# Split-precision pointwise product, stacked half slice in the down product, and a reordered first chunk, in a fused recurrent + FP4 feed-forward kernel

## The chip, the cores and the metric

One core of one Trainium2 chip. The metric is device time in microseconds (us) of one execution: the median of three runs is given, and beside it the span of one profiled execution, from its first to its last instruction.

## The reference

The input x has 16 sequences of 512 tokens with 256 features. With xn = layernorm(x), the kernel computes x + s * silu(f). All matrices are applied on the feature axis.

```python
# s: the recurrent branch
h  = dwconv3(rmsnorm(xn, g0)) + b           # 3 causal taps for each feature
x1 = h @ pw.T + b_pw + xn                   # "pointwise", 256 x 256
hidden, gate = split(rmsnorm(x1, g1) @ gru.T)          # 256 -> 512
x2 = minGRU(hidden, gate) + x1              # h_t = (1-z_t) h_(t-1) + z_t g(hidden_t)
s  = gelu(rmsnorm(x2, g2) @ w1.T + b1) @ w2.T + b2 + x2    # 256 -> 1024 -> 256
# f: the FP4 branch; q4 rounds to E2M1 in blocks of 16 with a scale for each block
hid = silu(q4(xn) @ q4(w_gate).T) * (q4(xn) @ q4(w_up).T)  # 256 -> 704
f   = q4(hid) @ q4(w_down).T                               # 704 -> 256
```

## The kernel before

A chunk is one sequence of 512 tokens; there are 16. `first()` does the first chunk and prepares the weights, `body(c, front)` is run for chunks 1 to 15 (`front` is false in the last), and `tail(15)` finishes. Every engine has its own hand-written order of steps (`first`, `body`, `tail` in each block), is strictly in order, and waits on semaphores. The loops are unrolled. In `body(c)` the FP4 branch's second half (quantise the hidden, transpose, `down`) and the second feed-forward product (`ff2`) of chunk c-1 run between `gate_up`, `gru` and `ff1` of chunk c; at the end of `body(c)` the front of chunk c+1 is made (`front_xc`, `front_xq`, `pointwise`).

Products that need near-float32 precision are made of float32r parts: each operand is held as a high part (ACT casts it to float32r) and a remainder (DVE subtracts), and `product` issues three matmuls: high x high, high x remainder, remainder x high. Only `pointwise` used plain float32 operands (`pw`, `y`): `product` then issues one float32 matmul, which the profile shows as two records. The names of a step's parts: `xs_hi/xs_lo` and `xslo_ready`, `act_hi/act_lo`, `xq_hi/xq_lo`, `hqt_hi/hqt_lo` and `hqtlo_ready`.

The 704 hidden features are five full slices of 128 and one half slice of 64 (`NFULL` = 5, `LAST` = 64, `KI` = 6). `hq` rows are 768 long, with zeros behind the 704 (set by POOL at the start), so that `down` runs six slices of 128 rows, 18 matmuls of 256 columns for each tile t of 128 tokens. DVE's steps for a tile are `hidden` (silu times up, L496), `fp4_scales`, `fp4_ratios`, `fp4_round`, `hidden_values` (L427, writes `hq`) and `hidden_low` (L519, writes `hqt_lo`).

The second rmsnorm of a chunk is a chain: DVE `recurrence` (both halves, L551 to L559), ACT `squares`, DVE `add_squares` (L524), PE `sum_squares` (L1042), DVE `clamp_sums` (L529, L531), POOL `rms_scale` (L348), PE `spread_scale` (L1050), DVE `scaled` (L539), ACT `high_part` (L799), DVE `scaled_low` (L545), PE `ff1`.

In `first()`, weights are quantised in six steps (`weight(0..5)` transposes, `weight_rest` subtracts the high part; `down_weight`, `down_rest` for the down matrix). `keep_busy(n)` issues n matmuls of the identity with no use but activity. The remainders of the gru, w1 and w2 weights are made by POOL (`low_weights`, L363).

Of the kernel before, what the change touches and what calls it, by code (L numbers as in the profile page):

```python
# [27 lines left out]
P = 128  # L28
# [31 lines left out]
def mixed_recurrent_kernel(nc, x, columns, pw_t, gru_t, w1_t, w2_t, w_gate, w_up, w_down, identity, out):  # L60
# [15 lines left out]
    with ctx:  # L76
# [17 lines left out]
        minus_ident = sb("minus_ident", [P, P], F32R)  # L94
# [7 lines left out]
        pw = sb("pw", [P, KD, D])  # L102
# [43 lines left out]
        w2_f, act_hi = shared_home(("w2_f", [P, KF * D + KD * NI], F32), ("act_hi", [P, KF, L], F32R))  # L146
# [5 lines left out]
        hqt_lo = sb("hqt_lo", [P, KI, P], F32R)  # L152
# [13 lines left out]
        dn_rows = w2_f[:, KF * D:KF * D + KD * NI].rearrange("p (k n) -> p k n", k=KD)  # L166
        w2_f = w2_f[:, 0:KF * D].rearrange("p (a n) -> p a n", a=KD)
        gru_f = keep[:, :, 0:2 * D]
# [12 lines left out]
        constants_ready = sem("constants_ready")  # L181
# [3 lines left out]
        wlo_ready = sem("wlo_ready")  # L185
        wq_ready = sem("wq_ready")
# [17 lines left out]
        y_ready = sem("y_ready")  # L204
        xqhi_ready = sem("xqhi_ready")
# [182 lines left out]
        def _(dve):  # L388
# [96 lines left out]

            def front_fp4_low(c):
# [28 lines left out]
            def hidden_low(c, t):  # L515
# [3 lines left out]
                V.tensor_tensor(hqt_lo[:], hqt_ps, hqt_hi[:].bitcast(F32), ALU.subtract).then_inc(hqtlo_ready, 1)  # L519
# [83 lines left out]
            def down_weight(e):  # L603

                if e == 0:
                    dve.wait_ge(constants_ready, 1)
                    dve.wait_ge(ld_dn, 16)
                dve.wait_ge(wqm_done, NFULL + e)
                quantise(dn_rows[:, e, :], hq[:, e, 0:NI], NBI).then_inc(wq_ready, 1)
# [3 lines left out]
            def first():  # L613
                front_moments(0)
                front_rows(0)
                front_fp4_values(0, front_fp4_ratios(0))
                front_taps(0)
                weight_values(0, weight_ratios(0, weight_scales(0)))
# [12 lines left out]
                scales = weight_scales(4)  # L631
                add_squares(1)
                weight_values(4, weight_ratios(4, scales))
                clamp_sums(1, gu_ps[:, 0, 0, :])
                weight_values(5, weight_ratios(5, weight_scales(5)))
                scaled(1, x1, gu_ps[:, 0, 1, :], (x2_ready, KD))
                scaled_low(1)
                down_weight(0)
# [9 lines left out]
                hidden(0, 3)  # L648
                ratios = fp4_ratios(hid[:, 0, :], NBI, hidden_scales(0, 0))
# [3 lines left out]
                hidden_low(0, 0)  # L653
                carried["ratios"] = fp4_ratios(hid[:, 1, :], NBI, hidden_scales(0, 1))
# [673 lines left out]
```

## Time and profile before

| what | value |
|---|---|
| median of 3 runs | 1087.53 us (1085.81 to 1088.24) |
| profiled execution: own time | 1085.26 us |
| profiled execution: span | 1083.5 us |
| granted TensorE clock, mean | 0.997 of full speed |
| PE / DVE / ACT / POOL busy | 1061.8 / 934.5 / 607.3 / 147.5 us |

A busy share tells how full an engine is; a view by time tells which of the engines a given wait ends on. Both are used below.

### The profile page before, as it was taken

How to read it: one execution, taken by the hardware profiler on the slowest of the kernel's cores; microseconds unless marked ns; L12 is line 12 of the kernel's file. 1: busy time of each engine (PE TensorE's matmuls, PEld its weight loads, DVE VectorE, ACT ScalarE, POOL GpSimd, SP SyncE). 2: the span in 40 equal slices, each digit the busy share in tenths (PEclk: the TensorE clock that was granted, in tenths of full speed). 3: DMA queues.
4: the chain of work that ended last, by engine and by line, in shares of the span. 5: the costliest groups of instructions: out<-in, count | busy, mean ns of one | idle time of the engine just before them, and what ended most of it. 6: DMA issues, size and time to landing. Idle time of an engine off the chain costs nothing. (4 is left out here: it accounts for less than half of the span.)

```text
span 1083.5 us, 18319 instructions
## 1 busy us (share of the span) xinstructions
PE 1061.8 (98%) x6954; PEld 967.9 (89%) x6954; DVE 934.5 (86%) x1720; ACT 607.3 (56%) x967; POOL 147.5 (14%) x123
## 2 busy tenths in 40 slices
PE   7899999999999999999999999999999999999998
PEld 6788989989898998989999898998989899898998
DVE  6978988989888898988889898898989889898895
ACT  5564464564746547474654747455574645647452
POOL 1230101112020110201111010111101011120010
PEclk9999999999999999999999999999999999999999
DMA  7000001010010101001010010101001010100110
GB/s 248 1 21 1 1 2 59 1 60 1 1 59 1 59 1 47 13 2 59 1 60 1 21 40 1 59 1 60 1 1 59 1 59 1 59 1 2 39 40 21
DMA packets 29365, 31.45 MB, mean 29 GB/s; under 512 B 1120, under 2 KB 28512, under 8 KB 29280
## 3 DMA queue, kind: packets, MB, share of 16 engines
q1 hardware_dynamic: 28448, 29.43, 8.7%
q8 instruction: 56, 0.92, 0.4%
q10 hardware_dynamic: 832, 0.87, 0.2%
q14 instruction: 29, 0.24, 0.1%
HBM read 21.90 MB, written 8.39 MB: 28 GB/s over the span
## 5 line engine op out<-in xcount | busy, mean ns | idle before, releaser
L990 PE MATMUL gu_ps<-gu_hi,xq_hi 128*128 128x352 f32 x512 | 168.3, 329 | 0.0
L990 PE MATMUL gu_ps<-gu_lo,xq_hi 128*128 128x352 f32 x512 | 165.9, 324 | 0.0
L990 PE MATMUL gu_ps<-gu_hi,xq_lo 128*128 128x352 f32 x512 | 165.7, 324 | 0.0
L990 PE MATMUL w_ps<-w_hi,act_hi 128*128 128x256 f32 x480 | 140.1, 292 | 0.0
L990 PE MATMUL w_ps<-w_hi,act_lo 128*128 128x256 f32 x480 | 135.1, 281 | 0.0
L990 PE MATMUL w_ps<-w_lo,act_hi 128*128 128x256 f32 x480 | 134.9, 281 | 0.0
L990 PE MATMUL w_ps<-dn_hi,hqt_hi 128*128 128x256 f32 x384 | 116.6, 304 | 2.0 <-DVE hqt_lo L519 2.0
L990 PE MATMUL w_ps<-dn_hi,hqt_lo 128*128 128x256 f32 x384 | 108.5, 283 | 0.0
L990 PE MATMUL w_ps<-dn_lo,hqt_hi 128*128 128x256 f32 x384 | 108.4, 282 | 0.0
L818 ACT ACTIVATE g<-w_ps 128x256 f32<-128x256 f32 x64 | 24.7, 385 | 147.7 <-PE w_ps L990 147.6
L496 DVE TENSOR_TENSOR hid<-sl,gu_ps 128x704 f32<-128x704 f32 x64 | 56.8, 887 | 58.8 <-PE gu_ps L990 58.2
L990 PE MATMUL gu_ps<-xs_hi,w_hi 128*128 128x512 f32 x256 | 102.5, 400 | 0.4 <-DVE xs_lo L545 0.4
L990 PE MATMUL gu_ps<-xs_lo,w_hi 128*128 128x512 f32 x256 | 101.0, 395 | 0.0
L990 PE MATMUL gu_ps<-xs_hi,w_lo 128*128 128x512 f32 x256 | 101.0, 395 | 0.0
L990 PEld LDWEIGHTS gu_ps<-gu_hi,xq_hi 128*128 128x128 f32 x512 | 96.7, 189 | 0.2 <-issue 0.2
L990 PEld LDWEIGHTS gu_ps<-gu_lo,xq_hi 128*128 128x128 f32 x512 | 96.6, 189 | 0.0
L990 PEld LDWEIGHTS gu_ps<-gu_hi,xq_lo 128*128 128x128 f32 x512 | 96.3, 188 | 0.0
L842 ACT ACTIVATE act<-gu_ps,cols 128x512 f32<-128x512 f32 x128 | 86.1, 687 | 13.7 <-PE gu_ps L990 13.3
L812 ACT CAST hqt_hi<-w_ps 128x768 fp32r<-128x768 f32 x64 | 51.3, 802 | 73.0 <-PE w_ps L1058 72.2
L356 POOL TENSOR_TENSOR o<-o,x_res 128x1024 f32<-128x1024 f32 x15 | 36.1, 2403 | 400.8 <-issue 393.4
L990 PEld LDWEIGHTS w_ps<-w_lo,act_hi 128*128 128x128 f32 x480 | 90.6, 189 | 0.0
L990 PEld LDWEIGHTS w_ps<-w_hi,act_hi 128*128 128x128 f32 x480 | 90.4, 188 | 0.0
(136 smaller groups left out, 2703.6 us busy)
## 6 DMA issues: line engine op xcount, KB each, us to landing
x_in<-x_dram SPq DMA_DIRECT2D x16, 512.0 KB, 5.8
x_res<-x_dram SPq DMA_DIRECT2D x16, 512.0 KB, 5.0
out_dram<-o SPq DMA_DIRECT2D x15, 512.0 KB, 3.5
act<-w_t_dram SPq DMA_DIRECT2D x1, 1024.0 KB, 11.3
w_f<-w_t_dram SPq DMA_DIRECT2D x1, 1024.0 KB, 13.8
w_f<-w_down_dram SPq DMA_DIRECT2D x1, 704.0 KB, 9.4
hid<-w_gate_dram SPq DMA_DIRECT2D x1, 640.0 KB, 5.9
hid<-w_up_dram SPq DMA_DIRECT2D x1, 640.0 KB, 9.3
```

Source lines behind the costliest of these rows:

```text
L356: nc.gpsimd.tensor_tensor(o[:], o[:], x_res[:], ALU.add).then_inc(out_ready, 1)
L496: V.tensor_tensor(hid[:, t, :].rearrange("p (h n) -> p h n", h=2), sl[:], gu_ps[:, 1, :, 0:HALF], ALU.mult).then_inc(hid_ready, 1)
L812: A.copy(hqt_hi[:], hqt_ps).then_inc(hqthi_ready, 1)
L818: A.activation(g[:, t, :], bank[:, 0:D], ACT.Silu).then_inc(g_ready, 1)
L842: A.activation(act1[:, j, :], ff1_bank(j), ACT.Gelu, bias=b1c[:, j:j + 1]).then_inc(gelu_ready, 1)
L990: done = M.matmul(psum, l, r, start=first and i == 0, stop=last and i == len(terms) - 1)
```

## The change

1. **Pointwise.** `pw` becomes `pw_hi` (cast by ACT in `first`) and `pw_lo` (subtracted by DVE in `first`); `y` gets `y_hi` (ACT, `front_y_high`) and `y_lo` (DVE, `front_y_low`) in every chunk. `pointwise` calls `product` with pairs.
2. **Down.** `hidden_values` writes the last 64 hidden features twice, into both halves of the last slice, in a second instruction. `hidden_low` leaves the remainder of the five full slices in `hqt_lo` (now five slices), and puts the half slice's remainder into rows 64 to 127 of the last slice of `hqt_hi`, in a second instruction over 64 partitions. `down` then covers the half slice with two matmuls: 64 rows of high x remainder weight, and 128 rows of (high, remainder) x (high weight, high weight). `down` has 17 matmuls.
3. **Body order.** PE does `front_xc(c + 1)` ahead of `ff1` and not in its middle. ACT does `front_y(c + 1)` after the first gelu and `front_y_high(c + 1)` ahead of the last two. DVE does `front_taps` ahead of `front_fp4_values`, then `front_y_low`.
4. **First chunk.** w1 and w2 remainders are made by DVE (`ff_low(1)`, `ff_low(2)`). Weight steps 3 to 5 move behind the second `spread_scale`, between the tiles of `ff1(0)`; `gelus_high(0, ...)` moves behind `hq_columns(0, 0)` and around `silu_f(0, 0)`; `front_xq(1)` comes ahead of `pointwise(1)`. The counts of `keep_busy` change.
5. **Homes.** `gru_f` is kept in `o`, `pw_f` behind `w2_f`, `y_hi` in `keep`'s place, `y_lo` in `cand`'s, `minus_ident` in `hqt_lo`; POOL's zeroing of `hq` is gone.

```diff
+        pw_hi = sb("pw_hi", [P, KD, D], F32R)
+        pw_lo = sb("pw_lo", [P, KD, D], F32R)
...
+        keep, y_hi = shared_home(("keep", [P, KD, L], F32), ("y_hi", [P, KD, L], F32R))
+        cand, y_lo = shared_home(("cand", [P, KD, L], F32), ("y_lo", [P, KD, L], F32R))
...
             def first():
                 layernorm_scales(0, 1)
-                low_weights(0)
+                gru_low()
                 rms_scale(0)
-                pool.wait_ge(xslo_ready, KD)
-                low_weights(1)
                 rms_scale(1)
-                pool.wait_ge(xslo_ready, 2 * KD)
-                low_weights(2)
                 layernorm_scales(1, 3)
...
+            def fp4_hidden_values(dst, rounded):
+                n, last = NBI * FP4_BLOCK, NFULL * P // FP4_BLOCK
+                fp4_values(dst[:, 0:n], NBI, rounded)
+                return V.scalar_tensor_tensor(blocks(dst[:, n:KI * P], NBI - last),
+                                              blocks(q_m[:, NFULL * P:n].bitcast(BF16), NBI - last),
+                                              1.0 / UNIT, spread(q_scale[:, last:NBI], NBI - last),
+                                              ALU.mult, ALU.mult)
...
+            def front_y_low(c):
+                for k in range(KD):
+                    dve.wait_ge(yhi_ready, KD * c + k + 1)
+                    V.tensor_tensor(y_lo[:, k, :], y[:, k, :], y_hi[:, k, :].bitcast(F32),
+                                    ALU.subtract).then_inc(ylo_ready, 1)
...
-                V.tensor_tensor(hqt_lo[:], hqt_ps, hqt_hi[:].bitcast(F32), ALU.subtract).then_inc(hqtlo_ready, 1)
+                V.tensor_tensor(hqt_lo[:], hqt_ps[:, 0:NFULL, :], hqt_hi[:, 0:NFULL, :].bitcast(F32), ALU.subtract)
+                twin = hqt_hi[LAST:P, NFULL, :]
+                V.tensor_tensor(twin, hqt_ps[LAST:P, NFULL, :], twin.bitcast(F32),
+                                ALU.subtract).then_inc(hqtlo_ready, 1)
...
+            def ff_low(j):
+                _, src, hi, lo = split_weights[j]
+                for k in range(KD):
+                    dve.wait_ge(whi_ready, KD * j + k + 1)
+                    V.tensor_tensor(lo[:, k, :], src[:, k, :], hi[:, k, :].bitcast(F32),
+                                    ALU.subtract).then_inc(flo_ready, 1)
...
             def first():
                 front_moments(0)
+                dve.wait_ge(pwhi_ready, 1)
+                V.tensor_tensor(pw_lo[:], pw_f, pw_hi[:].bitcast(F32), ALU.subtract).then_inc(pwlo_ready, 1)
                 front_rows(0)
...
-                weight_values(0, weight_ratios(0, weight_scales(0)))
+                scales = weight_scales(0)
+                front_y_low(0)
+                weight_values(0, weight_ratios(0, scales))
...
-                ratios = weight_ratios(2, weight_scales(2))
+                scales = weight_scales(2)
                 scaled(0, x1, w_ps[:, 1, :], (x1_ready, KD))
+                ratios = weight_ratios(2, scales)
+                scaled_low(0)
                 weight_values(2, ratios)
-                scaled_low(0)
-                weight_values(3, weight_ratios(3, weight_scales(3)))
+                ff_low(1)
                 recurrence(0, 0)
                 recurrence(0, 1)
...
                 hidden(0, 3)
+                front_y_low(1)
...
                 hidden_low(0, 0)
+                ff_low(2)
                 carried["ratios"] = fp4_ratios(hid[:, 1, :], NBI, hidden_scales(0, 1))
...
-                    front_fp4_values(c + 1, front_fp4_ratios(c + 1))
+                    ratios = front_fp4_ratios(c + 1)
                     front_taps(c + 1)
+                    front_fp4_values(c + 1, ratios)
+                    front_y_low(c + 1)
...
+            def front_y_high(c):
+                for k in range(KD):
+                    act.wait_ge(y_ready, KD * c + k + 1)
+                    act.wait_ge(pw_done, KD * c)
+                    act.wait_ge(x2_ready, KD * c)
+                    A.copy(y_hi[:, k, :], y[:, k, :]).then_inc(yhi_ready, 1)
...
                 hq_columns(0, 0)
+                gelus_high(0, range(KF // 2))
                 silu_f(0, 0, w_ps[:, 2, :])
+                gelus_high(0, range(KF // 2, KF))
...
-                for j in range(KF // 2):
+                gelus(c, (0,))
+                if front:
+                    front_y(c + 1)
+                gelus_high(c, (0,))
+                for j in range(1, KF // 2):
                     gelus(c, (j,))
                     gelus_high(c, (j,))
                 if front:
-                    front_y(c + 1)
-                    gelus(c, range(KF // 2, KF))
+                    gelus(c, range(KF // 2, KF - 2))
+                    front_y_high(c + 1)
+                    gelus(c, range(KF - 2, KF))
...
-                    pe.wait_ge(y_ready, KD * (c + 1))
+                    pe.wait_ge(yhi_ready, KD * (c + 1))
+                    pe.wait_ge(ylo_ready, KD * (c + 1))
...
-                        last = product(w_ps[:, e, :], pw[:, k, e * P:(e + 1) * P], y[:, k, :], False, k == KD - 1)
+                        last = product(w_ps[:, e, :], (pw_hi[:, k, e * P:(e + 1) * P], pw_lo[:, k, e * P:(e + 1) * P]),
+                                       (y_hi[:, k, :], y_lo[:, k, :]), False, k == KD - 1)
...
-                for k in range(KI):
-                    last = product(bank[:, 0:D], (hqt_hi[:, k, :], hqt_lo[:, k, :]),
-                                   (dn_hi[:, k, :], dn_lo[:, k, :]), k == 0, k == KI - 1)
-                last.then_inc(dn_done, 1)
+                for k in range(NFULL):
+                    product(bank[:, 0:D], (hqt_hi[:, k, :], hqt_lo[:, k, :]), (dn_hi[:, k, :], dn_lo[:, k, :]),
+                            k == 0, False)
+                M.matmul(bank[:, 0:D], hqt_hi[0:LAST, NFULL, :], dn_lo[0:LAST, NFULL, :], start=False, stop=False)
+                M.matmul(bank[:, 0:D], hqt_hi[:, NFULL, :], dn_hi[:, NFULL, :], start=False,
+                         stop=True).then_inc(dn_done, 1)
...
                 ff2(c - 1, 2, w_ps[:, 2, :], (g_ready, T * c))
-                ff1(c, range(KF // 2))
                 if front:
                     pe.wait_ge(sg_ready, T * c - 2)
                     front_xc(c + 1)
+                ff1(c, range(KF // 2))
+                if front:
                     ff1(c, range(KF // 2, KF))
```

## Rows read from the trace of the kernel before

**Rows 1.** The page: engine, busy us (share of the span), instructions.
```profile
PE 1061.8 (98%) x6954; PEld 967.9 (89%) x6954; DVE 934.5 (86%) x1720; ACT 607.3 (56%) x967; POOL 147.5 (14%) x123
```

**Rows 2.** Waits of PE: whom, us in total, times, longest.
```profile
PE gu_ps L1050 <- POOL inv_rms L348: 3.0, 14, 0.2
PE gu_ps L1109 <- issue: 1.7, 1, 1.7
```

**Rows 3.** Timeline of PE, pointwise, chunk 7: start us, us, engine, line, instruction.
```profile
545.58 0.60 PE L1013 MATMUL w_ps<-ident,xn 128*128 128x128 f32 x4
546.01 1.88 PE L990 MATMUL w_ps<-cand,pw 128*128 128x512 f32 x4
547.73 0.60 PE L1013 MATMUL w_ps<-ident,xn 128*128 128x128 f32 x4
```

**Rows 4.** Timeline of PE, a `down` of 18, then `gru`; a product behind transposes.
```profile
507.82 0.28 PE L990 MATMUL w_ps<-dn_hi,hqt_hi 128*128 128x256 f32 x1
...
509.96 0.39 PE L990 MATMUL gu_ps<-xs_hi,gru_hi 128*128 128x512 f32 x1
...
512.05 0.39 PE L990 MATMUL gu_ps<-xs_hi,gru_hi 128*128 128x512 f32 x1
...
522.80 0.36 PE L990 MATMUL w_ps<-dn_hi,hqt_hi 128*128 128x256 f32 x1
523.00 0.27 PE L990 MATMUL w_ps<-dn_lo,hqt_hi 128*128 128x256 f32 x1
```

**Rows 5.** Timeline of DVE, chunk 7; in brackets its idle time and what ended it.
```profile
486.23 3.09 DVE L512 TENSOR_TENSOR act_lo<-act,act_hi 128x512 fp32r<-128x512 f32 x5
492.18 0.89 DVE L496 TENSOR_TENSOR hid<-sl,gu_ps 128x704 f32<-128x704 f32 x1 [2.86 <-PE gu_ps L990]
...
503.13 0.89 DVE L496 TENSOR_TENSOR hid<-sl,gu_ps 128x704 f32<-128x704 f32 x1 [0.34 <-PE gu_ps L990]
...
520.78 0.95 DVE L519 TENSOR_TENSOR hqt_lo<-w_ps,hqt_hi 128x768 fp32r<-128x768 f32 x1
521.65 0.68 DVE L524 TENSOR_TENSOR xs<-xs 128x512 f32<-128x512 f32 x1
522.25 0.42 DVE L566 TENSOR_TENSOR o<-w_ps,g 128x256 f32<-128x256 f32 x1
523.08 0.69 DVE L529 TENSOR_REDUCE ss_sum<-gu_ps 128x4 f32<-128x512 f32 x1 [0.41 <-PE gu_ps L1042]
```

**Rows 6.** Timeline of PE, second rmsnorm of chunk 7.
```profile
522.21 0.28 PE L990 MATMUL w_ps<-w_hi,act_lo 128*128 128x256 f32 x1
522.39 0.66 PE L1042 MATMUL gu_ps<-ident,xs 128*128 128x128 f32 x4
...
525.39 0.65 PE L1050 MATMUL gu_ps<-ident,inv_rms 128*128 128x128 f32 x4 [0.22 <-POOL inv_rms L348]
```

**Rows 7.** Timeline of DVE and of ACT, end of chunk 7 (front of chunk 8).
```profile
538.81 1.22 DVE L427 SCALAR_TENSOR_TENSOR xq<-q_e,q_scale 128x1024 f32<-128x1024 bf16 x1
...
541.57 1.97 ACT L842 ACTIVATE act<-gu_ps,cols 128x512 f32<-128x512 f32 x3
...
546.55 2.20 ACT L807 CAST act_hi<-act 128x512 fp32r<-128x512 f32 x4
```

**Rows 8.** Timeline of DVE, first chunk and start of the second.
```profile
36.32 1.87 DVE L403 TENSOR_SCALAR q_wide<-q_amax 128x32 f32<-128x32 f32 x1
...
42.58 0.68 DVE L551 SCALAR_TENSOR_TENSOR cand<-gu_ps,cand 128x512 f32<-128x512 f32 x1
...
119.25 0.89 DVE L496 TENSOR_TENSOR hid<-sl,gu_ps 128x704 f32<-128x704 f32 x1 [0.34 <-PE gu_ps L990]
```

**Rows 9.** Timeline of PE, first chunk: gru, ff1.
```profile
35.95 0.47 PE L990 MATMUL gu_ps<-xs_hi,gru_hi 128*128 128x512 f32 x1 [1.96 <-DVE xs_lo L545]
...
59.13 0.47 PE L990 MATMUL gu_ps<-xs_hi,w_hi 128*128 128x512 f32 x1 [0.44 <-DVE xs_lo L545]
```

**Rows 10.** Timeline of POOL, first chunk.
```profile
35.77 4.75 POOL L363 TENSOR_TENSOR w_lo<-act,w_hi 128x1024 fp32r<-128x1024 f32 x2 [5.96 <-DVE xs_lo L545]
```

More of the change, by code:

```diff
@@ L151, in mixed_recurrent_kernel @@
         hqt_hi = sb("hqt_hi", [P, KI, P], F32R)
-        hqt_lo = sb("hqt_lo", [P, KI, P], F32R)
+        hqt_lo = sb("hqt_lo", [P, NFULL, P], F32R)
         q_amax = sb("q_amax", [P, 64])
@@ L166, in mixed_recurrent_kernel @@
         dn_rows = w2_f[:, KF * D:KF * D + KD * NI].rearrange("p (k n) -> p k n", k=KD)
+        pw_f = w2_f[:, KF * D + KD * NI:KF * D + KD * NI + KD * D].rearrange("p (k n) -> p k n", k=KD)
         w2_f = w2_f[:, 0:KF * D].rearrange("p (a n) -> p a n", a=KD)
-        gru_f = keep[:, :, 0:2 * D]
+        minus_ident = hqt_lo[:, 0, :]
+        gru_f = o[:].rearrange("p t d -> p (t d)").rearrange("p (k n) -> p k n", k=KD)
         gu_rows = hid[:].rearrange("p t n -> p (t n)")[:, 0:WT * D].rearrange("p (t d) -> p t d", d=D)
@@ L883, in first @@
                 act.wait_ge(ld_const, 32)
-                A.activation(minus_ident[:], ident[:], ACT.Copy, scale=-1.0).then_inc(minus_ready, 1)
+                A.activation(minus_ident, ident[:], ACT.Copy, scale=-1.0).then_inc(minus_ready, 1)
                 act.wait_ge(small_ready, 1)
+                act.wait_ge(ld_pw, 16)
+                A.copy(pw_hi[:], pw_f).then_inc(pwhi_ready, 1)
                 front_xc(0)
@@ L889, in first @@
                 high_weights(0)
+                front_y_high(0)
                 front_xq(0)
@@ L1146, in weight_rest @@
                 for i, (hi, bank) in enumerate(places):
-                    last = M.matmul(bank, minus_ident[:], hi, start=False, stop=i == len(places) - 1)
+                    last = M.matmul(bank, minus_ident, hi, start=False, stop=i == len(places) - 1)
                 last.then_inc(wqm_done, 1)
@@ L1173, in down_rest @@
                     n = min(4, KI - k)
-                    last = M.matmul(hqt_ps[:, k:k + n, :], minus_ident[:], dn_hi[:, k:k + n, e * P:(e + 1) * P],
+                    last = M.matmul(hqt_ps[:, k:k + n, :], minus_ident, dn_hi[:, k:k + n, e * P:(e + 1) * P],
                                     start=False, stop=True)
@@ L1203, in first @@
                 weight_rest(2)
+                keep_busy(24, w_ps[:, 0, :])
+                sum_squares(1, gu_ps[:, 0, 0, :], (coef_ready, 1))
+                keep_busy(8, w_ps[:, 0, :])
+                spread_scale(1, gu_ps[:, 0, 1, :], (cand_ready, 1))
                 weight(3)
-                weight_rest(3)
-                keep_busy(20, w_ps[:, 0, :])
-                sum_squares(1, gu_ps[:, 0, 0, :], (coef_ready, 1))
-                weight(4)
-                keep_busy(7, w_ps[:, 0, :])
-                spread_scale(1, gu_ps[:, 0, 1, :], (cand_ready, 1))
-                weight_rest(4)
-                weight(5)
                 keep_busy(8, w_ps[:, 0, :])
                 pe.wait_ge(whi_ready, 2 * KD)
-                pe.wait_ge(wlo_ready, 2 * KD)
-                ff1(0, range(1))
+                pe.wait_ge(flo_ready, KD)
+                ff1(0, (0, 1))
+                weight_rest(3)
+                ff1(0, (2,))
+                weight(4)
+                ff1(0, (3,))
+                weight_rest(4)
+                ff1(0, (4,))
+                weight(5)
+                ff1(0, (5,))
                 weight_rest(5)
-                ff1(0, range(1, KF // 2))
+                ff1(0, (6, 7))
                 down_weight(0)
-                ff1(0, range(KF // 2, KF))
-                down_rest(0)
                 pe.wait_ge(wqlo_ready, NFULL + 1)
                 gate_up(0, 0, 0)
-                down_weight(1)
+                down_rest(0)
                 gate_up(0, 0, 1)
                 gate_up(0, 1, 0)
+                down_weight(1)
+                gate_up(0, 1, 1)
                 down_rest(1)
-                gate_up(0, 1, 1)
                 front_xc(1)
@@ L1232, in first @@
                     gate_up(0, t, 1)
-                pointwise(1)
                 pe.wait_ge(hid_ready, T)
                 front_xq(1)
+                pointwise(1)
                 hq_transposes(0, 0, (dnlo_ready, KD))
```

75 lines of the change are left out of this document (37 added, 38 removed).

## The prediction

> **What bounds the kernel now.** I read the page's busy shares first. PE is busy 98% of the span, DVE 86%, ACT 56% [rows 1]: time can only leave if PE's stream gets shorter or its few waits go. The waits of PE come next: in the steady chunks there is one kind, 14 waits of at most 0.2 us for POOL's inverse root [rows 2]. So a matmul taken out should show in the end, unless DVE, the second fullest engine, can't follow. That needs the timeline of one steady chunk, and there the reader is to see where DVE is ahead of PE and where it is not. It is ahead by 2.86 us at the first `hidden` of a body and by 0.34 us at the third, and from 503.13 us to 523.08 us it has no wait at all [rows 5]. At the end of that stretch its `add_squares` ends near 522.33 (0.68 us from 521.65) and PE's `sum_squares` starts at 522.39, where the pitch of the matmuls alone gives 522.33 [rows 5, 6]. So in every chunk PE and DVE arrive at the second rmsnorm together; behind it comes a fixed chain, DVE, POOL, PE, whose end at `spread_scale` PE already awaits for 0.22 us [rows 6]. I split a chunk there: stretch A from `spread_scale` over the front of the next chunk to the third `hidden`, set by PE; stretch B from the third `hidden` to `spread_scale`, set by DVE and the chain.
>
> **Pointwise, PE.** One half (four transposes, two products) takes 547.73 - 545.58 = 2.15 us, 0.43 of it transposes, so two float32 products take 1.72 [rows 3]. In float32r a 512-column matmul follows the last after (512.05 - 509.96) / 9 = 0.232 us [rows 4]; six are 1.39 us. The half falls to 1.82, the chunk by 0.66 us; I take 0.64. The first float32r matmul behind transposes holds its successor up by 0.08 (523.00 - 522.80 = 0.20 for 0.12) [rows 4]; if that is not in the 0.43 already, the gain is 0.48. All of it lies in stretch A.
>
> **Down, PE.** 18 matmuls take 509.96 - 507.82 = 2.14 us, 0.119 each [rows 4]. One fewer saves 0.12 us, four times a chunk: the second of a body (tile 1 of the chunk before) and the first tile in stretch A, two in stretch B. No row shows a matmul of 64 rows. From below its extra cost is nothing, since 256 columns stream as before. The nearest row is the change from transposes to products: 0.08 us once [rows 4], which would leave 0.04 of the 0.12. From above: the array empties before and behind it; a matmul is there 0.28 us at a pitch of 0.12 [rows 4], so 0.16 for each change of form, 0.32 in all, or a loss of 0.20 for a `down`; and if the weight load (967.9 / 6954 = 0.14 us in the mean [rows 1]), otherwise overlapped, stands open at each change too, 0.60, or a loss of 0.48. I take nothing, as no change between the kinds of work in the rows costs more than 0.08, and keep both ends.
>
> The Trainium skill, TensorEngine Tiling (Array Packing), Key Properties, says that a change of tiling mode drains the engine, and a product over 64 rows may be such a change. By that rule the saving in `down` becomes the loss worked out above, the sum moves from -8.4 us to about +2; no row here can show it, every matmul stands as 128*128.
>
> **DVE's additions.** An instruction of DVE costs about 0.07 us and a column of 128 lanes about 1.04 ns: `hqt_lo` with 768 columns has a pitch of 521.65 - 520.78 = 0.87, five of 512 columns take 3.09, some 0.60 each [rows 5]. `front_y_low`: two of 512, 1.2 us a chunk, in stretch A. `hidden_values`: 64 more columns and one more instruction, 0.14 us, four times. `hidden_low`: 640 + 128 columns are the same 768, one instruction more, 0.07 us, four times. Bounds for the small ones: 0 if they overlap wholly, 0.42 each as for the shortest full-width row, `o` with 256 columns [rows 5]; the latter is hardly reached by a fourth of the columns. Together 2.0 us a chunk; DVE has 149 us idle in 16 chunks, 9 each [rows 1], so as a sum they fit. What counts is the place.
> - Stretch A: `y_low` comes where DVE then still is ahead at the first `hidden`: of 2.86 us [rows 5], 1.2 go for `y_low`, about 0.3 for the small ones and 0.88 because PE comes sooner. About 0.5 us of lead is left. Nothing lost, no wait of PE.
> - The third `hidden` has 0.34 us of lead [rows 5]; `hidden_values` takes 0.14 and the shorter `down` 0.12. It stays with PE by less than 0.1.
> - Stretch B: `hidden_low`, `hidden_values`, `hidden_low` stand between the third `hidden` and `add_squares`: 0.07 + 0.14 + 0.07 = 0.28 us, with no lead. The end of the stretch comes 0.28 later, and the two shorter `down` in it save nothing, PE waits some 0.4 us at `sum_squares` and 0.3 at `spread_scale`.
>
> **Order in the body.** `front_taps` now stands ahead of the 1.22 us `xq` values that ended at 540.03; about 3 us of taps put them at 543.2, for eight transposes that start 0.87 us (0.43 for four [rows 3]) ahead of pointwise, at 544.7. ACT's `y_high` follows the second gelu of the row at 541.57, thus 542.9, two casts of 0.55 end at 544.0 [rows 7]; `y_low` ends near 544.8, and pointwise starts at 545.58 [rows 3]. A cover of 0.8 us: if it is gone, PE waits ahead of pointwise for what is over. `front_xc` ahead of `ff1` only changes places with it. Behind PE's wait stand `down` and the next chunk's `gate_up`. No DMA moves in the body; `SP`'s queue has the same order. POOL only loses instructions; what stood behind its two subtractions (`rms_scale(1)`, the layernorm of chunk 1) waits for DVE's sums as before.
>
> **Steady sum.** Stretch A: -0.64 - 0.12 - 0.12 = -0.88; stretch B: +0.28. Together -0.60 us for each of the 13 intervals from chunk 1's `spread_scale` to chunk 14's: -7.8 us.
>
> **Last chunk.** Interval 14 to 15: -0.88, and -0.12 as DVE has no front to make there: -1.0. In the tail PE waited 1.7 us for DVE's remainders ahead of `ff2` [rows 2]; three `hidden_values` and one `hidden_low` more make that later by 0.49, and three shorter `down` behind it give 0.36 back: +0.1.
>
> **First chunk.** `pw_lo` (0.6 us) and `y_low` (1.2) are new ahead of the first rmsnorm, but two weight steps move behind it, so `gru` starts about 1.2 us later than 35.95 [rows 9]. Then POOL's 4.75 us subtraction no longer runs beside DVE [rows 10]; it stretched DVE's `q_wide` of 32 columns to 1.87 us [rows 8], where a price of 0.07 and 1.04 ns a column makes 0.1; two instructions of DVE find room in those 4.75 us, so I take 3.5 us in all. DVE's own subtraction costs 4 x 0.60 = 2.3 us. The recurrence starts at 41 to 42 for 42.58 [rows 8], a weight step of 2.7 us (three or four passes over 512 columns at 0.6 and small ones) has left the way behind it, and `ff1` starts near 56.3 for 59.13 [rows 9]. Of these 2.8 us, 1.2 go where `down_rest(0)`, before it hid between `ff1` tiles, now is PE's. Behind the gates `y_low` and the w2 subtraction (2.3) hold DVE, and ACT's eight casts of `act_hi` at 0.55 [rows 7], which formerly filled its gaps, wait for the latter: the gate's silu of chunk 1 comes last behind them, `hidden(1, 0)` is DVE's to be late with, and the third `hidden` of chunk 1 lands at 119.3 for 119.25 [rows 8]. With stretch B: +0.3 us. This walk has a dozen steps; I give it -3 to +2.
>
> **Sum.** +0.3 - 7.8 - 1.0 + 0.1 = -8.4 us. The profiled execution has a span of 1083.5 and a time of 1085.26, 2.3 below the median of 1087.53; the same difference on each gives 1075.1, 1076.9 and **1079.1 us** for the median.
>
> **Rivals.**
> 1. *DVE takes nothing back.* If `add_squares` has room that the timeline hides, PE's whole saving shows: 15 x 0.64 + 64 x 0.12 = 17.3 us, 1070. For it: PE at 98%. Against: the 20 us of DVE without a wait. It needs additions under 0.1 us.
> 2. *A small price for 64 rows*, 0.08 us: stretch A gives 0.16 less in 14 intervals, 0.3 in the tail: -5.8, 1081.7.
> 3. *The array empties* (0.32 us): `down` loses 0.20. Stretch A -0.24, stretch B still +0.28 at `sum_squares`, the next loss fits the 0.22 wait: about 0 a chunk, +1 to +2 in all: 1088 to 1090. No change.
> 4. *Slower*: emptying and an open weight load, a loss over 0.25 us for each `down`, decides; at the upper bound of 0.48 stretch A has -0.64 + 0.96 = +0.32, stretch B 0.96 less the 0.28 of waits that it has now, +0.68: 1.0 a chunk, 15 us in the steady chunks and 1 in the tail, 1103. For it: the weight loads, which have no other cover than the matmul before. Against: the switches that rows show cost 0.08.
> 5. *The first chunk is worse*, a wait for `wqm_done` or the half clock behind a gap: 3 us given up, 1082.
>
> **How the numbers follow.** Forecast as worked out 0.45; rival 1 0.11; rival 2 0.16; rival 5 0.06; rival 3 0.12; rival 4 0.10. 0.2% is 2.2 us, what this measurement can tell. Faster: 0.45 + 0.11 + 0.16 + 0.06 = 0.78; same 0.12; slower 0.10. The forecast's own range is 1076 to 1082.5 (first chunk -3 to +2, 0.48 or 0.64 for pointwise, small DVE instructions at 0 or twice the price). To leave out no more than 2 in 10, it must reach to rival 1 and to rival 3: 1070 to 1089.
>
> **What the changed profile would show.** Right: pointwise half 1.82 us; `down` 17 matmuls in 2.02 us; DVE `y_low` at 0.6; the chunk's period down by 0.60 from (503.13 - 119.25) / 6 = 63.98, the third `hidden` of chunk 7 against that of chunk 1 [rows 5, 8]; a new wait of PE at `sum_squares` of 0.3 to 0.5 us in chunks 1 to 14. Wrong: a gap beside the 64-row matmul; a wait ahead of pointwise for `y_low`; no wait at `sum_squares`; the third `hidden` of chunk 1 off 119.3 by more than 2.

## Result, and the profile after: slower by 1.1%

The changed kernel takes 1097.91 us (median of 4 runs, 1097.36 to 1100.12) beside 1087.62 for the kernel before: ratio 1.0111, 95% interval 1.0095 to 1.0126. The forecast was 1079.1, faster; even the range, up to 1089, did not hold it. The profiled execution took 1098.24 us with a span of 1096.5 at a granted clock of 0.998, 13.0 us above the span before.

The page's first part, after (engine, busy us, share, instructions), answers to [rows 1]:

```profile
PE 1072.4 (98%) x6982; PEld 981.5 (90%) x6982; DVE 976.6 (89%) x1887; ACT 618.7 (56%) x1000; POOL 138.1 (13%) x118
```

PE's busy time rose by 10.6 us although each half of pointwise became shorter and each `down` has a matmul less: something in PE's stream costs more. Its waits after (whom, us, times, longest), against [rows 2]:

```profile
PE gu_ps L1099 <- DVE xs L540: 4.1, 14, 0.3
PE gu_ps L1168 <- issue: 1.9, 1, 1.9
```

The wait at `sum_squares` (L1099) is there 14 times, as forecast, and the one for POOL's inverse root has shrunk to 0.4 us in all; 4.1 and 0.4 for the 3.0 of before, 1.5 us more and no explanation of 13. So the next view is PE's timeline. The end of one `down` in the body of chunk 7, its last four matmuls and the first of `gate_up`, with two of the weight loads (PEld):

```profile
502.40 0.28 PE L1045 MATMUL w_ps<-dn_lo,hqt_hi 128*128 128x256 f32 x1
502.40 0.19 PEld L1045 LDWEIGHTS w_ps<-dn_hi,hqt_lo 128*128 128x128 f32 x1
502.52 0.28 PE L1045 MATMUL w_ps<-dn_hi,hqt_lo 128*128 128x256 f32 x1
502.73 0.18 PEld L1125 LDWEIGHTS w_ps<-dn_lo,hqt_hi 64*128 64x128 f32 x1
502.73 0.38 PE L1125 MATMUL w_ps<-dn_lo,hqt_hi 64*128 64x256 f32 x1
503.04 0.38 PE L1126 MATMUL w_ps<-dn_hi,hqt_hi 128*128 128x256 f32 x1
503.26 0.32 PE L1045 MATMUL gu_ps<-gu_hi,xq_hi 128*128 128x352 f32 x1
```

The reader is to look at the starts, not the durations. The pitch is 0.12 us until the matmul of 64 rows; that one starts 0.21 behind its predecessor, the next 0.31 behind it, the next 0.22. Over the regular 0.12 these are 0.09, 0.19 and 0.10: **0.38 us for one matmul of 64 rows among matmuls of 128**, against the 0.12 us that the matmul taken out saves. A `down` is 0.26 us longer, not 0.12 shorter.

The weight loads say more. Inside the stream a load starts with the matmul ahead of its own, 0.12 us before it is wanted (502.40 for the matmul at 502.52). The load of the 64-row matmul starts at 502.73, together with that matmul, and the load behind it starts together with its own at 503.04; both matmuls last 0.38 us for 0.28. So at both changes the weight load stands open, which rival 4 named. How the price divides between an array that empties and an open load is not shown.

Pointwise, chunk 9 (starts of the two halves and of what follows), against [rows 3]:

```profile
615.43 0.60 PE L1069 MATMUL w_ps<-ident,xn 128*128 128x128 f32 x4
...
617.27 0.60 PE L1069 MATMUL w_ps<-ident,xn 128*128 128x128 f32 x4
...
619.12 0.28 PE L1045 MATMUL w_ps<-dn_hi,hqt_hi 128*128 128x256 f32 x1
```

A half is 1.84 us (forecast 1.82, before 2.15). Its gain of 0.62 us a chunk is there.

DVE from the third `hidden` of chunk 7 to `add_squares`, against [rows 5]:

```profile
507.40 0.89 DVE L508 TENSOR_TENSOR hid<-sl,gu_ps 128x704 f32<-128x704 f32 x1 [0.47 <-PE gu_ps L1045]
...
510.88 0.76 DVE L531 TENSOR_TENSOR hqt_lo<-w_ps,hqt_hi 128x640 fp32r<-128x640 f32 x1
511.65 0.29 DVE L534 TENSOR_TENSOR hqt_hi<-w_ps,hqt_hi 64x128 fp32r<-64x128 f32 x1
511.98 1.29 DVE L561 TENSOR_TENSOR xs_lo<-xs,xs_hi 128x512 fp32r<-128x512 f32 x2
...
516.73 0.22 DVE L435 SCALAR_TENSOR_TENSOR hq<-q_e,q_scale 128x64 f32<-128x64 bf16 x1
516.86 1.40 DVE L444 BATCH_NORM_STATS2 stats<-x_in 128x6 f32<-128x256 f32 x4
...
525.49 0.82 DVE L531 TENSOR_TENSOR hqt_lo<-w_ps,hqt_hi 128x640 fp32r<-128x640 f32 x1
526.32 0.29 DVE L534 TENSOR_TENSOR hqt_hi<-w_ps,hqt_hi 64x128 fp32r<-64x128 f32 x1
526.64 0.69 DVE L540 TENSOR_TENSOR xs<-xs 128x512 f32<-128x512 f32 x1
```

From `hidden` to `add_squares` it is 526.64 - 507.40 = 19.24 us; before, 521.65 - 503.13 = 18.52 [rows 5]. The 0.72 more: the second `hidden_low` has a pitch of 526.64 - 525.49 = 1.15 where one instruction took 0.87 (0.28 more), the first 1.10 for 0.81 there (0.29), the values 0.13. Neighbouring instructions of 128 lanes overlap by some 0.08 in most places: `hq` with 64 columns starts 0.81 after an instruction of 0.89. (Not where one reads what the one ahead wrote, as in the recurrence: 519.58 follows 518.86 by 0.72, for a duration of 0.68.) The one on 64 lanes reads nothing that its predecessor writes, and still doesn't overlap: it starts 0.77 and 0.83 after instructions of 0.76 and 0.82, and its successor 0.33 and 0.32 after it, though it has only 128 columns and lasts 0.29.

The two stretches of the prediction, from the timelines of DVE (L508, the third `hidden`) and PE (L1107, `spread_scale`):

```profile
572.24 0.89 DVE L508 TENSOR_TENSOR hid<-sl,gu_ps 128x704 f32<-128x704 f32 x1 [0.47 <-PE gu_ps L1045]
```
```profile
595.23 0.65 PE L1107 MATMUL gu_ps<-ident,inv_rms 128*128 128x128 f32 x4
```
```profile
636.88 0.89 DVE L508 TENSOR_TENSOR hid<-sl,gu_ps 128x704 f32<-128x704 f32 x1 [0.46 <-PE gu_ps L1045]
```

The period is 636.88 - 572.24 = 64.64 us (63.98 before). Stretch B is 595.23 - 572.24 = 22.99 where it was 525.39 - 503.13 = 22.26: +0.73. Stretch A is 41.65 where it was 63.98 - 22.26 = 41.72: -0.07, which is -0.62 for pointwise and about +0.54 for two `down`.

The ends of the program, third `hidden` of chunk 1 and of chunk 15:

```profile
119.61 0.89 DVE L508 TENSOR_TENSOR hid<-sl,gu_ps 128x704 f32<-128x704 f32 x1 [0.48 <-PE gu_ps L1045]
...
1024.96 0.89 DVE L508 TENSOR_TENSOR hid<-sl,gu_ps 128x704 f32<-128x704 f32 x1 [0.46 <-PE gu_ps L1045]
```

Before, the first stood at 119.25 [rows 8], and the last was

```profile
1014.95 0.89 DVE L496 TENSOR_TENSOR hid<-sl,gu_ps 128x704 f32<-128x704 f32 x1 [0.34 <-PE gu_ps L990]
```

So the 13.0 us are: first chunk +0.36; fourteen intervals, 905.35 - 895.70 = +9.65 (fourteen of 0.65 are 9.1; two intervals are 0.2 and 0.3 longer); from there to the end, 71.54 for 68.55, +3.0. In this tail PE's wait ahead of `ff2` was 1.95 us for 1.74 and ended at 1070.93 and 1060.03. The stretches of 28 matmuls behind it (the windows view: us, then busy time of each engine, the granted clock, DMA share, GB/s), first after, then before:

```profile
1071.20:1075.60 4.40, 4.40 (x28) 4.40 (x27) 4.11 (x10) 0.32 (x1) 0.00 (x0) 0.69 0.00 0
```
```profile
1060.20:1063.30 3.10, 3.10 (x28) 3.10 (x28) 3.00 (x7) 0.61 (x2) 0.00 (x0) 1.00 0.02 5
```

The granted clock has a mean of 0.69 there after the longer wait, thus part of the stretch at the level of 1.2 GHz, and 1.00 before: 4.4 us for 3.1, 1.3 of the tail's 3.0. The trace has the lower level from 1070.48, still inside the wait, to 1073.89.

The length of the wait alone is not what decides. With `down` of before and three 64-row matmuls (an experiment below) the wait at this place was 1.41 us and ended at 1074.99, and the clock fell:

```profile
1075.20:1078.60 3.40, 3.40 (x18) 3.40 (x17) 3.30 (x7) 0.90 (x2) 0.00 (x0) 0.51 0.02 5
```

With one such matmul it was 1.36 and the clock stayed at 1.00, as it did behind 1.77 in the kernel with pointwise alone, and behind the wait of 2.15 us that ends at 99.14 in the changed kernel itself.

Of the two longer intervals, that from chunk 7 to 8 can be followed. ACT, with no wait for another engine, is late by 0.28 us:

```profile
545.69 0.62 ACT L850 CAST act_hi<-act 128x512 fp32r<-128x512 f32 x1 [0.39 <-ACT act L885]
```

`y_hi`, `y_low` and pointwise (550.77) pass it on, and PE loses 0.2. The kernel with pointwise alone has the same 0.19 in the same interval. What held ACT is not shown.

### The profile page after: what moved, and what is told of

Same layout as the page of the kernel before. It is cut to its first block, busy times and chain, and to the rows that moved or that the text cites. A ratio compares the mean times of both kernels' runs of the same rounds, so it can differ in the third digit from the quotient of the medians.

```text
span 1096.5 us, 18651 instructions
## 1 busy us (share of the span) xinstructions
PE 1072.4 (98%) x6982; PEld 981.5 (90%) x6982; DVE 976.6 (89%) x1887; ACT 618.7 (56%) x1000; POOL 138.1 (13%) x118
## 4 chain that ended last, share of the span: by engine, by line
PE 68%; DVE 26%; issue 4%; DMA 1%; ACT 1%; POOL 0%; ACTq 0%; DVEq 0%
PE gu_ps L1045 35%; PE w_ps L1045 20%; DVE xs L572 3%; DVE hqt_lo L531 2%; PE w_ps L1115 2%; DVE cand L570 2%; DVE xs L555 2%; DVE stats L444 2%; DVE cand L567 2%; DVE hid L508 1%; DVE xs_lo L561 1%; DVE q_amax L402 1%; PE w_ps L1126 1%; PE w_ps L1125 1%; DVE q_y L414 1%
## 5 line engine op out<-in xcount | busy, mean ns | idle before, releaser
L1045 PE MATMUL w_ps<-dn_hi,hqt_hi 128*128 128x256 f32 x320 | 94.0, 294 | 2.6 <-DVE hqt_hi L534 2.6
L1045 PEld LDWEIGHTS w_ps<-w_hi,act_lo 128*128 128x128 f32 x480 | 90.4, 188 | 0.0
L1045 PE MATMUL w_ps<-dn_hi,hqt_lo 128*128 128x256 f32 x320 | 90.0, 281 | 0.0
L1045 PE MATMUL w_ps<-dn_lo,hqt_hi 128*128 128x256 f32 x320 | 89.9, 281 | 0.0
```

The lines of the kernel that those rows point to most:

```text
L1045: done = M.matmul(psum, l, r, start=first and i == 0, stop=last and i == len(terms) - 1)
```

## Experiments

Theory E: the 64-row matmul costs 0.38 us of PE wherever it stands (the array empties), the 64-lane subtraction 0.28 us of DVE in stretch B, and pointwise gives its 0.6 us a chunk undiminished. Rivals were that the loss is the stacking itself (its extra work on DVE, whatever the rows), and that pointwise or the new order takes its gain back. All periods below are from third `hidden` to third `hidden` in steady chunks. The kernels of one group ran together; ratios are to the kernel before in the same group (medians 1087.72, 1085.22 and 1085.86 us in the three groups), and are what may be compared across groups.

### The remainder's matmul over all 128 rows

```
-M.matmul(bank[:, 0:D], hqt_hi[0:LAST, NFULL, :], dn_lo[0:LAST, NFULL, :], start=False, stop=False)
+M.matmul(bank[:, 0:D], hqt_hi[:, NFULL, :], dn_lo[:, NFULL, :], start=False, stop=False)
```

It adds the product of the two remainders to the sum, a term that neither kernel has.

> The changed kernel with the remainder-weight product of the half slice over all 128 rows (17 matmuls, none of 64 rows). Theory (the array empties around a matmul of 64 rows, 0.38 us for each down): the last two matmuls follow at 0.12 us, a down takes 2.02 us for 2.41, the chunk's period falls from 64.63 to 63.87 us, since only the two down of stretch A save 0.38 each and stretch B stays with DVE; wait of PE at sum_squares 0.6 to 0.7 for 0.29; median 1085 to 1087. Rival (it is the in-place rows of hqt_hi, written by DVE, or the end of the group that holds the last matmuls up): gaps of 0.2 to 0.3 us remain, median 1097.

1085.85 us, ratio 0.9986 (0.9975 to 0.9998); period 63.87. PE, end of a `down` and start of `gru`, then the second rmsnorm:

```profile
573.54 0.28 PE L1125 MATMUL w_ps<-dn_lo,hqt_hi 128*128 128x256 f32 x1
573.66 0.29 PE L1126 MATMUL w_ps<-dn_hi,hqt_hi 128*128 128x256 f32 x1
573.78 0.39 PE L1045 MATMUL gu_ps<-xs_hi,gru_hi 128*128 128x512 f32 x1
...
586.98 0.66 PE L1099 MATMUL gu_ps<-ident,xs 128*128 128x128 f32 x4 [0.67 <-DVE xs L540]
```

The pitch is 0.12 throughout, though the rows written in place and the end of the group are as before: that rival is out. One matmul's row range changed, 64 rows to 128, and 12 us are gone: 64.64 - 63.87 = 0.77 a chunk, two times 0.38 in stretch A. In stretch B the price had been covered by DVE: now PE waits 0.67 us for `add_squares` where it waited 0.3.

### The remainder subtraction over 128 lanes as well

```
+V.memset(fold[0:LAST, :], 0.0)
+V.memset(fold[LAST:P, :], -1.0)
...
-twin = hqt_hi[LAST:P, NFULL, :]
-V.tensor_tensor(twin, hqt_ps[LAST:P, NFULL, :], twin.bitcast(F32), ALU.subtract)
+twin = hqt_hi[:, NFULL, :]
+V.scalar_tensor_tensor(twin, twin.bitcast(F32), fold[:, 0:1], hqt_ps[:, NFULL, :], ALU.mult, ALU.add)
```

On top of the last kernel. In this form rows 0 to 63 of the slice are written too: they get their value from PSUM once more, again as float32r.

> As rows128, and the remainder of the half slice made over 128 lanes: hi * (0 or -1 by row) + hqt_ps, so that rows 0 to 63 are rounded again and rows 64 to 127 get the remainder. Theory (an instruction over 64 lanes does not overlap its neighbours on DVE: 0.28 us more for hidden_low and not 0.07): hidden_low costs 0.87 + 0.07, stretch B shortens by 2 x 0.2 = 0.4 us, period 63.45, median 1079 to 1081. Rival (any second instruction after the first one costs 0.28): the period stays at that of rows128.

1081.64 us, ratio 0.9946 (0.9929 to 0.9962); period 63.54, each just above what was expected. DVE, a `hidden_low` in front of `add_squares`:

```profile
582.32 0.82 DVE L532 TENSOR_TENSOR hqt_lo<-w_ps,hqt_hi 128x640 fp32r<-128x640 f32 x1
583.05 0.34 DVE L535 SCALAR_TENSOR_TENSOR hqt_hi<-hqt_hi,fold,w_ps 128x128 fp32r<-128x128 f32 x1
583.31 0.68 DVE L541 TENSOR_TENSOR xs<-xs 128x512 f32<-128x512 f32 x1
```

The longer instruction, over twice the lanes, has the shorter pitch: 0.73 and 0.26 for 0.83 and 0.32, together 0.99 for 1.15. Two of them make 0.32 us, and the period fell by 0.33. Stretch B is 22.65 for 23.00, stretch A is unchanged. So DVE's split sets stretch B. That the second instruction writes a tile that the first reads is not the reason for the lost overlap: it does so here too. Still 0.12 more than the undivided instruction's 0.87.

### The kernel before with 64-row matmuls alone

One of `down`'s 18 matmuls over 64 rows, and then all three of the last slice; rows 64 and up of `hq` there are zeros, the result is the same:

```
-M.matmul(..., hqt_hi[:, NFULL, :], dn_lo[:, NFULL, :], ...)
+M.matmul(..., hqt_hi[0:LAST, NFULL, :], dn_lo[0:LAST, NFULL, :], ...)
```

> The kernel before, its down still of 18 matmuls, only that high x remainder weight of the half slice runs over 64 rows. Theory (0.38 us for one matmul of 64 rows among those of 128): a down takes 2.14 + 0.38 = 2.52 us, stretch A gets 0.76, stretch B 0.3 to 0.5 longer, period 65.1 to 65.3, median 1105 to 1108. Rival (the gaps come from the stacked operand): no change, 1087.6.

> The kernel before with all three matmuls of the half slice over 64 rows, at the end of each down. Theory (the price is of the two changes of form, not of the matmul): a down takes 2.5 us as in before_64, period 65.0, median 1102. Rival (every matmul of 64 rows pays 0.19 us, as it is not pipelined with its neighbour): a down takes 2.9 us, period 66 or more, 1117.

One: 1102.22 us, ratio 1.0135 (1.0118 to 1.0152), period 65.01; the median is 3 us under what was expected, the period just under its band. Three: 1103.32 us, ratio 1.0172 (1.0155 to 1.0189), period 65.02. PE with one, then with three:

```profile
570.36 0.28 PE L1068 MATMUL w_ps<-dn_hi,hqt_hi 128*128 128x256 f32 x1
570.57 0.38 PE L1069 MATMUL w_ps<-dn_lo,hqt_hi 64*128 64x256 f32 x1
570.88 0.39 PE L1070 MATMUL w_ps<-dn_hi,hqt_lo 128*128 128x256 f32 x1
571.10 0.32 PE L990 MATMUL gu_ps<-gu_hi,xq_hi 128*128 128x352 f32 x1
```
```profile
580.42 0.28 PE L990 MATMUL w_ps<-dn_hi,hqt_lo 128*128 128x256 f32 x1
580.63 0.38 PE L990 MATMUL w_ps<-dn_hi,hqt_hi 64*128 64x256 f32 x1
580.85 0.28 PE L990 MATMUL w_ps<-dn_lo,hqt_hi 64*128 64x256 f32 x1
580.97 0.28 PE L990 MATMUL w_ps<-dn_hi,hqt_lo 64*128 64x256 f32 x1
581.18 0.50 PE L990 MATMUL gu_ps<-xs_hi,gru_hi 128*128 128x512 f32 x1
```

The same 0.21, 0.31, 0.22 as in the changed kernel, with nothing else changed; stretch A is 0.75 longer than before, two times 0.38, and stretch B 0.28. With three, 0.21, 0.22, 0.12, 0.21, and the 512-column matmul behind has 0.34 to its successor (581.52) where 0.23 is regular: 0.09, 0.10, 0, 0.09 and 0.11, again 0.39 in all. (The two ratios lie further apart than their intervals allow, the periods do not: the two ran in different groups, and the lower clock in the tail of the second makes that tail 71.5 us for 70.1.) The price belongs to each change of the row count, about 0.19: 0.09 ahead of the first matmul of the new form and 0.10 behind it. It does not grow with the number of matmuls in between.

### Pointwise and the new order alone, down as before

```
-hqt_lo = sb("hqt_lo", [P, NFULL, P], F32R)
+hqt_lo = sb("hqt_lo", [P, KI, P], F32R)
...
-fp4_hidden_values(hq[:, t % 2, :], rounded)
+fp4_values(hq[:, t % 2, 0:NI], NBI, rounded)
...
-(17 matmuls, one over 64 rows)
+for k in range(KI): last = product(bank[:, 0:D], (hqt_hi[:, k, :], hqt_lo[:, k, :]), ...)
```

POOL's zeroing of `hq` is back with it.

> The changed kernel with the down part undone (18 matmuls, hq padded with zeros, one hidden_low and one hidden_values instruction): pointwise split, body order and first chunk as changed. Theory (the pointwise part alone gains its 0.64 us, the down part lost it): period 63.98 - 0.64 = 63.34, h of the first chunk as before, median 1077 to 1080. Rival (y_low and y_high cost DVE and PE more than they bring): period 63.9 or more, 1087.

1077.0 us (1076.93 to 1077.47), ratio 0.9903 (0.9887 to 0.992), period 63.37; third `hidden` of chunk 1 at 119.15, of chunk 15 at 1006.7, and a tail of 68.5 us as before. It is faster than both kernels. Pointwise gives 63.98 - 63.37 = 0.61 us a chunk, and nothing comes back. It also beats the kernel with 128 rows and 128 lanes (1081.64, run on the same chip beside it, whole ranges apart): the stack itself, with no price for rows left, gives PE 0.12 us for each `down` and takes more than that from DVE. Its stretch A is 0.22 shorter than here and its stretch B 0.39 longer.

### The statistics of the next chunk earlier in DVE's order

With stretch B set by DVE, its 2.0 us of `front_moments(c + 1)`, which stand in it, were moved to stretch A; once on the last kernel, once on that with 128 rows and lanes:

```
 gelus_low(c - 1, range(5))
+if front:
+    front_moments(c + 1)
 hidden(c, 0)
...
 hidden_values(c - 1, 3, fp4_round(NBI, ratios))
-if front:
-    front_moments(c + 1)
 recurrence(c, 0)
```

> old_down with DVE's front_moments(c + 1), 2.0 us, moved from ahead of the recurrence to ahead of the body's first hidden. Theory (stretch B is set by DVE only up to sum_squares, where PE is 0.06 us early, and by the chain behind it): the period falls by 0.05 to 0.1 from 63.37, median 1076 to 1077. Rival (DVE sets all of stretch B): a gain of up to 2 us a chunk, 1050. Other way: the first hidden has about 0.7 us of lead, and if PE's gates wait for it, the period rises by up to 1.3.

> lanes128 with the same move. Theory (the stacked down can pay as soon as DVE has room ahead of add_squares): the wait of PE at sum_squares, 0.39 us in 14 chunks, goes, the one at spread_scale (0.34) stays; period 63.54 - 0.39 = 63.15, median 1075 to 1077, at or below old_down_early. Rival (later hidden hold the gates up): 1081 or more.

1229.62 us (ratio 1.1326, 1.1307 to 1.1345) and 1231.65 us (1.1353, 1.1334 to 1.1372): a miss by 150 us. First the waits of DVE (whom, us, times, longest), then SyncE's queue in the one with the old `down`:

```profile
DVE stats L446 <- DMA x_in<-x_dram: 128.3, 13, 10.8
```
```profile
549.96 0.40 SPq L315 DMA_DIRECT2D out_dram<-o  x1
...
551.17 0.84 SPq L311 DMA_DIRECT2D x_in<-x_dram  x1
```

The load of `x_in` stands behind the store of the chunk before in SyncE's order, and that waits for POOL's `o`. In the old order the statistics came late enough not to notice. To test this, the loop of SyncE got the load first:

```
 with sp.Fori(0, B - 3) as i:
-    store(i)
     load(i + 3)
+    store(i)
```

once alone, and once under each of the two kernels with early statistics.

> The kernel with the pointwise part alone, and in SyncE's loop the load of chunk i+3's x issued ahead of the store of chunk i. In the trace of old_down SyncE issues o's store at 553.84, x_res at 554.42 and the x_in load at 555.05, though xn, the last reader of x_in, ended near 522: the load has stood some 31 us behind the store's wait. A control: x_in is first read at 572.9 there, so the earlier load by itself should change nothing. Queue theory: ratio as that of old_down (0.990), period 63.37 +- 0.1, span 1075 +- 1.5. Rival (the earlier transfer collides with something): slower by 1 us or more, with the same instructions slowed in every chunk.

> old_down_early with the same swap. Queue theory of why old_down_early lost 152 us: its statistics waited 10.8 us in each chunk for x_in, whose load stood behind the store of the chunk before; with the load ahead of the store it is issued near 525, some 40 us before the statistics of the next chunk want it, so the wait of DVE for x_in goes from 128 us to under 2 and the time falls back from 1230 to 1075 to 1078. Rival (the order of DVE's work itself was the cause): it stays above 1150. Whether the earlier statistics then gain anything: period 63.3 (gain of 0.07, from the wait for inv_rms) or 63.37 as before, median within 2 us of old_down_swap either way.

> lanes128_early with the same swap: down's stacked last product over all 128 rows, the half slice's remainder over 128 lanes, statistics ahead of hidden(c, 0). Queue theory: back from 1232 to 1077 to 1082; lanes128 had 1081.6 and period 63.54. If the 0.36 us a chunk that down's one matmul less saves on PE is only held back by the waits of sum_squares and spread_scale for DVE (5 us each in 14 chunks), and early statistics shorten these, period 63.15 to 63.4 and 1075 to 1079, as fast as old_down; rival (DVE's own total sets stretch B, wherever the statistics stand): period 63.5, 1081 to 1082, and old_down_early2 stays the faster by 3 to 5 us.

The swap alone: 1076.78 us, ratio 0.9916 (0.9901 to 0.9931), period 63.37, no change. With early statistics: 1089.04 us, 1.0027 (1.0017 to 1.0038), period 64.17; and 1091.47 us, 1.0046 (1.0033 to 1.006), period 64.33. The queue theory holds for 140 of the 150 us, since the wait for `x_in` is gone. The last 12 were expected by neither theory of these two runs; the expectation of the first run with early statistics had named, as the other way, a period longer by up to 1.3 if PE comes to wait for DVE. It is 0.80 longer. DVE in chunk 7, early statistics:

```profile
516.34 0.69 DVE L565 SCALAR_TENSOR_TENSOR cand<-gu_ps,cand 128x512 f32<-128x512 f32 x1 [1.33 <-ACT cand L871]
```

and ACT, the same place:

```profile
515.71 0.60 ACT L871 ACTIVATE cand<-gu_ps 128x512 f32<-128x512 f32 x1
```

DVE's waits for this `cand` were 1.9 us in two places and are 20.1 us in 16. ACT ends it 9.81 + 0.60 us after the third `hidden` in either order (515.71 - 505.90 here, 509.18 - 499.37 with late statistics), so 1.33 of the 2.0 us given free in stretch B are spent waiting for ACT, and that stretch is only 0.11 shorter. All 2.0 are added to stretch A, where DVE had less than that to spare, and it is 0.91 longer. PE waits there for DVE, 15 times where it was twice (whom, us, times, longest):

```profile
PE w_ps L1044 <- DVE hqt_lo L533: 6.1, 15, 2.0
```

Where the statistics stood they filled the gap ahead of `cand`.

### The first chunk: w2's remainders back to POOL, later

On the kernel with the old `down`: POOL makes them after the layernorm of chunk 1.

```
 layernorm_scales(1, 3)
+w2_low()      # POOL: two tensor_tensor subtractions
...
-ff_low(2)     # DVE
```

> old_down with the w2 remainders made by POOL behind its layernorm of chunk 1, not by DVE behind hidden_low(0, 0). Theory (in the first chunk DVE's 2.36 us and ACT's casts behind it hold up chunk 1): third hidden of chunk 1 at 117.5 to 118.5 for 119.15, median 0.7 to 1.5 less than old_down, 1075.5 to 1076.3. Rival (POOL's subtraction stretches DVE's instructions beside it, as before): no gain, 1077.

1078.64 us, ratio 0.994 (0.9923 to 0.9956), period 63.35. The third `hidden` of chunk 1 is at 120.95, 1.8 us later instead of earlier. POOL ran its two at 73.30, 5.38 us in all, and PE had a wait of 2.5 us for DVE's `hid` that was not there before. DVE's instructions beside POOL's two are the reason:

```profile
73.43 3.02 DVE L438 SCALAR_TENSOR_TENSOR hq<-q_e,q_scale 128x704 f32<-128x704 bf16 x1
76.37 3.44 DVE L474 TENSOR_SCALAR xn<-x_in,moments,rstd 128x256 f32<-128x256 f32 x4
```

In the kernel with the old `down`, where POOL does nothing at this time, the same two take 0.89 and 1.38 us: 4.2 us longer, more than the subtraction that DVE no longer makes. So DVE is slowed beside POOL, as read from [rows 8, 10].

## Why the prediction was wrong

1. **What bounds the kernel** was right. PE's stream in stretch A, DVE and its chain in stretch B: after the change the two add up by their own sources, and the experiment on rows moved A alone, that on lanes B alone.
2. **Pointwise**: right, 1.84 us a half, 0.61 a chunk by the kernel that has it alone (forecast 0.64).
3. **Down, the step that failed.** "No row shows a matmul of 64 rows ... I take nothing, as no change between the kinds of work in the rows costs more than 0.08": it costs 0.38. The 0.08 of [rows 4] stands at a change from transposes to products, both over 128 rows, so it was no row of a change of the row count; and even as a stand-in it was counted once, where a lone matmul makes two changes. The bound of 0.32 for an array that empties was near, that of 0.60 with an open weight load not reached, although the loads do stand open (502.73 and 503.04). By the Trainium skill, TensorEngine Tiling (Array Packing), Key Properties, a change of tiling mode drains the engine. This trace fits that, with 0.19 us for each change between 128 and 64 rows, of which the part of the open load is not known. In the sum: stretch A -0.07 for -0.88, of which 0.77 is this term.
4. **DVE's small instructions.** `hidden_values` was right, 0.13 for 0.14. `hidden_low` was taken as 0.07 for one instruction more and is 0.28, as the one on 64 lanes overlaps nothing; twice in stretch B, +0.73 for +0.28. The bound of 0.42 held it. This is what rival 3 lacked: with emptying at 0.32 and +0.28 in stretch B it came to no change, with 0.38 and 0.73 the period is +0.65. Rival 4 was to decide from a loss over 0.25 for each `down`; the loss was 0.26, with the open weight load that it named, at about half of its upper price.
5. **The wait at `sum_squares`** came as forecast in place and number, 14 times 0.3 us, but the number was luck: DVE came 0.72 later for 0.28, and PE, with a 64-row matmul ahead of the wait, 0.26 later and not 0.12 earlier. The 0.3 forecast at `spread_scale` did not come (one wait, 0.4 us in all). In the kernel with 128 rows both waits are there, 14 times each, up to 0.7 and 0.4 us: DVE's lateness hid two of the four 64-row matmuls of a chunk.
6. **Cover ahead of pointwise**: forecast 0.8 us. `y_low` waits 1.1 us for ACT's `y_hi`. That stands behind the second gelu, as forecast, but starts 2.18 us ahead of pointwise where the forecast had 2.7: with `front_xc` now ahead of `ff1`, ACT's first gelu starts 9.73 us ahead of pointwise (605.70) for 10.62 before, and the forecast had that exchange cost nothing.

```profile
612.10 1.26 ACT L885 ACTIVATE act<-gu_ps,cols 128x512 f32<-128x512 f32 x2
613.25 1.14 ACT L800 CAST y_hi<-cand 128x512 fp32r<-128x512 f32 x2
```

   `y_low` ends at 615.19, pointwise starts at 615.43. Where PE does wait for `y_low` the two lie 0.15 apart, so 0.1 us is left; it was enough in all steady chunks but the one at 550.77.
7. **First chunk**: `gru` at 36.83 (forecast 37.15), the recurrence at 40.53 (41 to 42), `ff1` at 55.39 (56.3), the third `hidden` of chunk 1 at 119.61 (119.3). (4 x 0.60 for DVE's own subtraction is 2.4 and not 2.3; nothing hangs on it.) The gain was given back where it was said to be, in chunk 1's front, as PE's waits there show:

```profile
99.14 0.36 PE L1045 MATMUL w_ps<-dn_hi,hqt_hi 128*128 128x256 f32 x1 [2.15 <-DVE hqt_hi L534]
...
107.81 0.43 PE L1045 MATMUL gu_ps<-gu_hi,xq_hi 128*128 128x352 f32 x1 [1.01 <-ACT sl L836]
```

8. **Tail**: +3.0 us for +0.1. 1.3 of it is the lower clock around the wait of 1.95 us. The kernel with 128 rows, whose clock falls in the tail as well, takes 1.45 us less from the third `hidden` of chunk 15 to the end, so about that much is the 64-row matmuls.

With the two sizes put in (0.26 lost for each `down`, 0.28 for each `hidden_low`), the prediction's own sum is +0.7 for the first chunk, 13 x 0.61 = 7.9, +0.4 for the last interval and +1.5 for the tail: 10.5 us (each 0.61 is -0.09 in stretch A and +0.70 in stretch B). The lower clock adds 1.3 and the two longer intervals 0.5, which makes 12.3 of the 13.0 measured: the structure held and the prices did not. What stays open: the remaining 0.7 us, what held ACT in the interval from chunk 7 to 8, the other longer interval, and why the clock fell in this tail and not in that of before.

## What to carry to other kernels

A matmul with another row count inside a dense stream costs PE two changes of the row count, here 0.38 us, more than the three 256-column matmuls that 0.36 us of stream holds: keep the row count, or put all matmuls of one count side by side. When a price is not in the trace and its bounds differ in the sign of the result, the middle is no forecast; a chance of one in five for the bad end was too low where a written rule speaks for it.
An instruction split off on an engine that sets a stretch counts with the overlap that it loses, and one moved away counts with the gap that it filled; before moving a read forward, look where its transfer stands in the queue. The version to keep is pointwise in two float32r parts with `down` left as it was: 1077.0 us, 1% under the kernel before.

## What the runs showed of the hardware

- TensorE: each change between 128 and 64 rows costs 0.19 us (0.09 ahead, 0.10 behind the first of the new form), 0.38 for a lone matmul and 0.39 for a group of three. At a change the weight load starts with its own matmul, elsewhere in the stream 0.12 us ahead of it.
- DVE: 128 columns on 64 lanes took a pitch of 0.32 us and lost the overlap with the instruction ahead (0.83 for a duration of 0.82); 128 columns on 128 lanes 0.26 and 0.73. Half the lanes were slower. The two differ in the operation as well (subtract, multiply and add), so the number of lanes, the starting lane and the operation were not separated.
- DVE beside POOL's `tensor_tensor` (5.38 us for two of 128x1024): 3.02 us for an instruction of 0.89, 3.44 for four of 1.38 in all.
- The granted clock was at 1.2 GHz from 1070.48 to 1073.89 around a wait of PE of 1.95 us, fell near one of 1.41 us in another run, and stayed at 2.4 GHz behind waits of 1.36, 1.74, 1.77 and 2.15 us: the length of the last wait alone does not tell.
